# Relative attention: unshifted score rows are shifted from SBUF to SBUF, four partitions a transfer, instead of through a DRAM buffer

## The reference

```
AC = jnp.einsum('bhid,bhjd->bhij', q + u_bias[None, :, None, :], k)
BD = jnp.einsum('bhid,hjd->bhij', q + v_bias[None, :, None, :], rp)
BD = _rel_shift(BD)        # row i is moved left by an amount that depends on i
attn = jax.nn.softmax((AC + BD) * scale, axis=-1)
out = jnp.einsum('bhij,bhjd->bhid', attn, v)
```

## Time and profile before

| | |
|---|---|
| median of 3 runs | 2229.96 us (2224.44 to 2232.92) |
| profiled execution, its own time | 2224.83 us |
| its span | 2223.2 us |
| relative attention, first to last tile of DVE | 1202.6 to about 2079 us |
| one of its 32 steps | 27.4 us on average |

### The profile page before, as it was taken

The page is one execution under the profiler, slowest core; times in us unless marked ns, Lnnn a source line. Parts: engine busy times, 40 slices in busy tenths (PEclk is TensorE's granted clock), DMA queues, the critical chain, the costliest instruction groups (busy, mean ns, idle before and its releaser), DMA issues. The chain is left out here.

```text
span 2223.2 us, 56316 instructions
## 1 busy us (share of the span) xinstructions
PE 1591.8 (72%) x20267; PEld 1050.0 (47%) x20455; DVE 1321.3 (59%) x3147; ACT 1036.5 (47%) x1964; POOL 185.3 (8%) x281
## 2 busy tenths in 40 slices
PE   5433358788832999997624888787888787988547
PEld 2212136566621666664312555455555555656323
DVE  5764277566635666674321767576666665767546
ACT  4432226566620232321414767576666665766203
POOL 2322300000023000000210000000000000000013
PEclk8767669889965999998865989899998888989759
DMA  1114722222136212121789899999999999999441
GB/s 38 42 43 156 218 58 62 51 55 59 48 102 199 95 53 105 52 91 44 225 227 312 307 363 347 349 333 344 339 357 345 344 337 348 316 369 343 128 134 57
DMA packets 220937, 433.30 MB, mean 195 GB/s; under 512 B 54736, under 2 KB 116080, under 8 KB 211280
## 3 DMA queue, kind: packets, MB, share of 16 engines
q1 hardware_dynamic: 202928, 263.61, 39.4%
q10 hardware_dynamic: 12672, 152.05, 16.6%
q0 software_dynamic: 5088, 14.16, 2.1%
HBM read 225.93 MB, written 203.55 MB: 193 GB/s over the span
## 5 line engine op out<-in xcount | busy, mean ns | idle before, releaser
L2013 DVE CUSTOM_DVE_ANT_0 r_shifted<-r_ps_ac,r_shifted 128x512 f32<-128x512 f32 x512 | 352.1, 688 | 319.7 <-PE r_ps_ac L1890 157.5
L1979 ACT ACTIVATE r_probs<-r_ps_keys 128x512 f32<-128x512 f32 x512 | 309.6, 605 | 259.3 <-PE r_ps_keys L1897 225.8
L1897 PE MATMUL r_ps_keys<-r_ident,r_shifted 128*128 128x128 f32 x2048 | 334.0, 289 | 64.0 <-DMA r_v<-v 27.8
L1958 ACT ACTIVATE r_wide<-r_ps_wide 128x512 f32<-128x512 f32 (+1 forms) x576 | 329.7, 591 | 86.4 <-PE r_ps_wide L1881 85.0
L1897 PEld LDWEIGHTS r_ps_keys<-r_ident,r_shifted 128*128 128x128 f32 x2048 | 273.8, 149 | 54.2 <-issue 13.3
L1881 PE MATMUL r_ps_wide<-r_r,r_qv 48*32 48x64 bf16 (+12 forms) x6144 | 244.6, 259 | 65.7 <-issue 54.7
L2021 DVE TENSOR_SCALAR r_shifted<-r_shifted,r_mx 128x512 f32<-128x512 f32 x512 | 249.2, 487 | 18.3
L873 DVE TENSOR_REDUCE c_mx<-c_ps_rows 128x2 f32<-128x256 f32 (+3 forms) x256 | 197.7, 818 | 100.9 <-PE c_ps_rows L744 100.2
L846 ACT ACTIVATE c_probs<-c_ps_keys 128x512 f32<-128x512 f32 (+1 forms) x384 | 179.9, 530 | 140.6 <-PE c_ps_keys L744 137.2
L1881 PEld LDWEIGHTS r_ps_wide<-r_r,r_qv 48*32 48x32 bf16 x6144 | 105.9, 96 | 170.5 <-issue 168.7
L1357 ACT ACTIVATE e_silu<-e_ps_a 128x1024 f32<-128x1024 f32 x64 | 65.7, 1027 | 216.1 <-PE e_ps_a L1290 216.1
(11 more groups left out here) (197 smaller groups left out, 2084.5 us busy)
## 6 DMA issues: line engine op xcount, KB each, us to landing
skew<-r_wide ACTq DMA_DIRECT2D x64, 2224.0 KB, 12.1
r_shifted<-skew SPq DMA_DIRECT2D x64, 2048.0 KB, 18.3
e_weight_all<-weights SPq DMA_DIRECT2D x8, 2048.0 KB, 7.7
stack<-d_part SPq DMA_DIRECT2D x96, 128.0 KB, 2.6
stack<-b_part SPq DMA_DIRECT2D x48, 128.0 KB, 3.5
stack<-b_part POOLq DMA_DIRECT2D x48, 128.0 KB, 3.7
c_q<-stack SPq DMA_DIRECT2D x64, 96.0 KB, 2.2
c_k<-stack SPq DMA_DIRECT2D x64, 96.0 KB, 2.3
```

Source lines behind the costliest of these rows:

```text
L1897: last = pe.transpose(ps_keys[u % 2][:, j * P:(j + 1) * P], shifted[:, s, u, j * P:(j + 1) * P], ident[:, :])
L1958: act.activation(wide[:, s, c, lo:hi], ps_wide[bk % BANKS][:, 0:hi - lo], ACT.Copy).then_inc(wide_sb, 1)
L1979: act.activation(probs[:, h % 2, :, b * P:(b + 1) * P], ps_keys[u % 2][:, :].rearrange("p (j i) -> p j i", j=NT), ACT.Exp, scale=SCALE).th ...
L2013: dve.tensor_tensor_reduce(out=shifted[:, s, u, :], in0=ps_ac[u % 2][:, :], in1=shifted[:, s, u, :], scale=1.0, scalar=LOWEST, op0=ALU.add ...
```

## The change

The DRAM buffer goes. Each half of `wide` is copied by DMAs from SBUF to SBUF, straight into `shifted`. Rows at the same place i in the four strips (partitions i, i+32, i+64, i+96) need the same shift, so one transfer moves these four rows: 4 partitions x 8 tiles x 512 elements, 64 KB. A half takes 32 such transfers. SP's queue issues those of places 0, 16, 1, 17, ..., 7, 23, and GpSimd's queue those of places 8, 24, 9, 25, ..., 15, 31. GpSimd had no work in this phase before. Since the strips need no common pitch, their columns are no longer staggered, and `wide` has 4352 columns a half instead of 4448.

```
-CW = HT * W + P - Q
+    CW = HT * W
+    PLACES = [[i + o for i in range(Q // 4) for o in offsets] for offsets in ((0, 16), (8, 24))]
+    SKEW = 16 * Q // 2
+        tiles = wide[:, :, :, :].rearrange("p s c (v w) -> p s c v w", w=W)
...
+        def skew(eng, it, j, c, half, turned):
+
+            eng.wait_ge(wide_sb, 2 * NBK * (STEP * it + j) + NBK * (c + 1))
+            eng.sem_inc(skew_marks[half], 1)
+            if turned is not None:
+                eng.wait_ge(keys_ps, turned)
+                eng.sem_inc(skew_marks[half], 1)
+            for i in PLACES[half]:
+                at = Q - 1 - i
+                eng.dma_start(shifted[i::Q, j % 2, HT * c:HT * (c + 1), :], tiles[i::Q, j % 2, c, :, at:at + L])                    .then_inc(skewed[half][j % 2][c], 16)
+
+        def skew_step(eng, it, j, first, left, half):
+            n = STEP * it + j
+            if left >= 1:
+                skew(eng, *after(it, j, 1), 1, half, None if first else TG * n)
+            if left >= 2:
+                skew(eng, *after(it, j, 2), 0, half, TG * n + HT)
...
-            def fetch(it, j, c):
-
-                sp.wait_ge(sent[j % 2][c], 16 * uses(it, j))
-                src = skew_dram[j % 2][c]
-                sp.dma_start(shifted[:, j % 2, HT * c:HT * (c + 1), :],
-                             bass.AP(tensor=src.tensor, offset=src.offset + P - 1, ap=[[CW - 1, P], [W, HT], [1, L]]))\
-                    .then_inc(skewed[j % 2][c], 16)
...
-                if left >= 1:
-                    if not first:
-                        sp.wait_ge(keys_ps, TG * n)
-                    fetch(*after(it, j, 1), 1)
-                if left >= 2:
-                    sp.wait_ge(keys_ps, TG * n + HT)
-                    fetch(*after(it, j, 2), 0)
+                skew_step(sp, it, j, first, left, 0)
...
+        @block.gpsimd
+        def _(pool):
+            for c in range(2):
+                skew(pool, 0, 0, c, 1, None)
+            skew(pool, 0, 1, 0, 1, None)
+            steps(lambda it, j, first, left: skew_step(pool, it, j, first, left, 1), pool)
...
-                        start = W * v + P - Q - Q * a
+                        start = W * v
...
-            def send(n, s, c):
-                act.wait_ge(wide_sb, 2 * NBK * n + NBK * (c + 1))
-                dst = skew_dram[s][c]
-                act.dma_start(bass.AP(tensor=dst.tensor, offset=dst.offset, ap=[[CW, P], [1, CW]]),
-                              wide[:, s, c, :]).then_inc(sent[s][c], 16)
...
                         if bk == 0:
-                            act.wait_ge(sent[s][c], 16 * uses(it, j))
+                            for half in range(2):
+                                act.wait_ge(skewed[half][s][c], SKEW * uses(it, j))
...
                     if u % HT == 0:
-                        dve.wait_ge(skewed[s][u // HT], 16 * uses(it, j))
+                        for half in range(2):
+                            dve.wait_ge(skewed[half][s][u // HT], SKEW * uses(it, j))
```

More of the change, by code:

```diff
@@ L1704, in _, with phase_relative @@
             steps(step, dve)
-def phase_relative(nc, sems, qu_stacks, qv_stacks, k_stacks, v9_in, r_stack, ident_in, skew_dram, ctx_out):
+def phase_relative(nc, sems, qu_stacks, qv_stacks, k_stacks, v9_in, r_stack, ident_in, ctx_out):
     SCALE = DH ** -0.5
     BANK = 512
+    CW = HT * W
     NBK = -(-CW // BANK)
@@ L1754, in phase_relative @@
         wide_sb = sem("wide_sb")
-        sent = [[sem(f"sent{s}{c}") for c in range(2)] for s in range(2)]
-        skewed = [[sem(f"skewed{s}{c}") for c in range(2)] for s in range(2)]
+        skew_marks = [sem("skew_marks0"), sem("skew_marks1")]
+        skewed = [[[sem(f"skewed{half}{s}{c}") for c in range(2)] for s in range(2)] for half in range(2)]
         ac_ps = sem("ac_ps")
@@ L1781, in uses, with after @@
             return (STEP // 2) * it + j // 2 + 1
+        def after(it, j, by):
+            return it + (j + by) // STEP, (j + by) % STEP
+        def skew(eng, it, j, c, half, turned):
[13 more added lines that the diff above has]
+                skew(eng, *after(it, j, 2), 0, half, TG * n + HT)
         @block.sync
@@ L1795, in load_queries @@
                     .then_inc(qv_loaded[j % 2], 16)
-            def fetch(it, j, c):
-                sp.wait_ge(sent[j % 2][c], 16 * uses(it, j))
-                src = skew_dram[j % 2][c]
-                sp.dma_start(shifted[:, j % 2, HT * c:HT * (c + 1), :],
-                             bass.AP(tensor=src.tensor, offset=src.offset + P - 1, ap=[[CW - 1, P], [W, HT], [1, L]]))\
-                    .then_inc(skewed[j % 2][c], 16)
-            def after(it, j, by):
-                return it + (j + by) // STEP, (j + by) % STEP
             def step(it, j, first, left):
@@ L1841, in _ @@
             for c in range(2):
-                fetch(0, 0, c)
+                skew(sp, 0, 0, c, 0, None)
             sp.wait_ge(wide_ps, 2 * NBK)
             load_queries(0, 2)
-            fetch(0, 1, 0)
+            skew(sp, 0, 1, 0, 0, None)
             sp.wait_ge(wide_ps, 4 * NBK)
@@ L1853, in _ @@
                 for c in range(2):
-                    sp.wait_ge(sent[s][c], 16 * (NI // 2))
-                    sp.wait_ge(skewed[s][c], 16 * (NI // 2))
+                    for half in range(2):
+                        sp.wait_ge(skewed[half][s][c], SKEW * (NI // 2))
             sp.wait_ge(r_loaded, 32)
             sp.wait_ge(stored, 64 * (NI + 1))
+        @block.gpsimd
[4 more added lines that the diff above has]
+            steps(lambda it, j, first, left: skew_step(pool, it, j, first, left, 1), pool)
         @block.tensor
@@ L1988, in step @@
                             copy_wide(n + 2, s, c, HT)
-                            send(n + 2, s, c)
                     if u == 2 and not first:
@@ L1998, in _ @@
                         copy_wide(n, n, c, bk)
-                    send(n, n, c)
             steps(step, act)
@@ L2048, in program @@
     r_stack = dram("r_stack", (SK, H, 2 * L), BF16)
-    skew = [[dram(f"skew{s}_{c}", (P * CW,)) for c in range(2)] for s in range(2)]
     sems = Semaphores(nc)
@@ L2065, in program @@
     sems = Semaphores(nc, sems)
-    phase_relative(nc, sems, stacks[2], stacks[3], stacks[4], v9[1], r_stack, ident, skew, sums[1])
+    phase_relative(nc, sems, stacks[2], stacks[3], stacks[4], v9[1], r_stack, ident, sums[1])
     sems = Semaphores(nc, sems)
```

## The result

The changed kernel takes 2646.3 us (median of 4 runs, 2644.6 to 2652.6) against 2228.3 us before: 1.188 times, with a 95% interval of 1.183 to 1.193. The forecast was 2750 us, range 2260 to 3150. Slower was right, the size was 104 us too large. Full engines were rightly named, as the traces show, but they are not all that holds the kernel, and the prices of an issue and of GpSimd's traffic were wrong.

What follows compares the result with a forecast made beforehand. Transfers were taken to bound relative attention at 27.4 us a step. Four DMA engines with 701 KB at 16 GB/s give 43.8 us: 16.4 us more, x 32 = +525 on 2224.8, so 2750 us, range 2260 to 3150.

Steps and rivals of the forecast that it cites:

- What bounded the kernel before: Relative attention, 27.4 us a step, was held by its transfers (DMA engines 97% busy), mostly the detour through DRAM.
- What the change removes: 8.75 MB a step of DRAM write and read back, replaced by 4.19 MB; ACT's 21 us of issues worth nothing.
- No term: Stage's first tile: its new wait, 16 us for 1 MB through four engines, is about as long as write and fetch.
- Few DMA engines: A 4-partition transfer runs on 4 engines, the same four for all SP's transfers; each has 701 KB a step.
- Issuing: SP's 32 issues cost 9 to 13 us a step, GpSimd's 18.6 us, both inside the step.
- The rate: Each of the four engines moves 16 GB/s, hindered half of the time, so 701 KB take 43.8 us a step.
- rival 1: The four engines don't hinder each other: 29.2 us a step, +58 us, 2283 us; chance 0.17.
- the forecast's span: Steps between 29.2 us (engines unhindered) and 58.4 us (always hindering each other), given as 2286 to 3217 us.
- Sharing between partitions: Partitions 32 apart lie on one port; always in step, SP's half alone would take 38.5 us on two ports.
- 2: SP's transfers go round over all 16 engines; TensorE sets a 23.5 us step, -125 us, 2100 us; chance 0.17.
- 3: GpSimd's issues become the bound beside DVE's work; doubled to 1.16 us, 37.1 us a step, 2535 us; chance 0.07.
- The signs to look for: DMA share about a half, SP's landing times far beyond GpSimd's, DVE waiting for SP's half, step over 35 us.

Runs made afterwards that it cites:

- short transfers: Changed kernel with all 64 transfers a step issued, each moving 2 of its 8 tiles, 16 KB instead of 64 (scores wrong): 2101 us, 0.941 times.
- SP alone, 4 engines: Changed kernel without GpSimd's transfers, its places never shifted (scores wrong), SP's 32 transfers a step kept: 2323 us, 1.041 times.
- SP 8 places, GpSimd 24: Changed kernel with SP given 8 of the 32 places and GpSimd 24, right shifts: 2359 us, from one execution.
- GpSimd's transfers short: Changed kernel with GpSimd's 32 transfers a step cut to 2 of their 8 tiles, SP's whole (scores wrong): 2377 us, 1.069 times.
- another order of places: Changed kernel with SP's places ordered 0, 4, 16, 20, 1, ... and GpSimd's 8, 12, 24, 28, 9, ..., right shifts: 2479 us, 1.112 times.
- SP 12 places, GpSimd 20: Changed kernel with 12 places for SP, 20 for GpSimd, neighbouring transfers reaching other ports, right shifts: 2499 us, 1.120 times.
- partitions 4 apart: Changed kernel with SP's four partitions of a transfer 4 apart instead of 32, SP having places 0 to 15 (scores wrong): 2614 us, 1.172 times.
- SP's transfers on 16 engines: Changed kernel with each SP transfer reaching 16 partitions and 2 tiles instead of 4 and 8, still 64 KB (scores wrong): 2685 us, 1.204 times.
- the same, SP alone: SP's transfers of 16 partitions and 2 tiles, without any transfer of GpSimd (scores wrong): 2236 us, 1.006 times.

## Why the prediction was right, and where its reason failed

*What bounded the kernel before* stands: with few enough bytes (short transfers) the phase runs at 23.7 us a step instead of 27.4.

*What the change removes* stands: ACT did the same work in the same time, TensorE the same work in 1635 us instead of 1592, at a lower granted clock in this stage (0.76 instead of 0.89). The other phases hardly moved: the span grew by 421.8 us, of which 404.4 lie between DVE's first and last tile (1279.9 against 875.5) and 19.7 before the first, at 1222.3 instead of 1202.6 us, and behind them it is 2.3 shorter. Those 19.7 are a small miss: the forecast had "No term" there.

*Few DMA engines* stands as a count, exactly, and these engines are full. The Trainium skill's rule ("DMA: Bandwidth & Descriptors", Why a DMA increments its semaphore by 16 and not by 1) agrees with the four completions a transfer and with a share of 0.25 while more transfers wait; no run shows which four engines they are. What the four have to do in a step can be estimated from the packet records of 1400 to 2000 us: the durations of SP's 2048-byte packets over the engines that they run on, and those of all other packets of SP's and GpSimd's queues over 16, as if evenly spread.

| kernel | packet time of each of SP's engines, us a step | step, us |
|---|---|---|
| SP alone, 4 engines | 30 | 30.6 |
| SP 8 places, GpSimd 24 | 37 | 31.6 |
| GpSimd's transfers short | 33 | 32.2 |
| another order of places | 40 | 35.3 |
| SP 12 places, GpSimd 20 | 42 | 36.0 |
| partitions 4 apart | 46 | 39.1 |
| the changed kernel | 48 | 40.0 |
| SP's transfers on 16 engines | 26 | 41.0 |
| the same, SP alone | 11 | 27.9 |

In the first seven the packet time is about the step or over it (so packets must overlap in the records), as full engines would show, and with both queues' transfers whole a longer packet time goes with a longer step. It is no independent price, since the time of a packet of one size changes with the traffic beside it (GpSimd's 4 KB take 329 to 489 ns here). In the last two the engines are not full on average; the step is no shorter beside GpSimd's traffic, and 2.7 us shorter without it. So the forecast named a load that is there, but taking it away does not give a fast kernel; what then holds SP's queue stays open.

*Issuing* is a step that failed: "SP's 32 issues cost 0.28 us ... to 0.39 us: 9 to 13 us a step, inside the step". The rows that it rested on were other shapes. A 4 x 8 x 512 transfer takes 0.59 us from issue to issue, 18.9 us a step, and with the other issues SP's queue has 23.7 us of work of its own, as much as TensorE. Push-back comes on top of that at once; full engines and what hinders them have 16 us of the 40 us step to explain.

*The rate*: 16 GB/s for an engine was a guess for all traffic, and that 701 KB in 40.0 us are 17.5 GB/s is in part luck. Of the forecast's 43.8 us, SP's 524 KB were 32.8, and their packets took about 30; GpSimd's 131 KB were 8.2, and took about 14; loads and stores were 2.9, and took 3.6. The term that was mis-sized most is GpSimd's: 9.0 GB/s for a busy engine, near the lower bound of 8.9 from the earlier trace rows, where its half was given the same rate as SP's. In steps, the runs add up like this: 23.7 us for SP's queue with short transfers, + 6.9 for the length of SP's own transfers (SP alone, 30.6), + 9.4 for GpSimd's transfers beside them (40.0), of which 7.8 go with three quarters of their bytes; a better order of places gives back 4.7. How a full engine reaches back to the queue that issues is argued from these differences and from the DMA shares; the trace does not show it. A slip without weight: 29.2 us a step is 2283 us, as under rival 1, not the 2286 at the low end of the forecast's span.

*Sharing between partitions* matters where it was not looked for. Among SP's transfers it is worth 1.2 us a step as measured, with dearer issues against it; among GpSimd's, several of which are under way at once, busy engines run at 7.5 GB/s with nothing else beside them and at 11.2 in another order. That fits the Trainium skill's port map ("SBUF — State Buffer", Door 1: The DMA port swizzle): 32 apart is the same port, and places 8, 24, 9, 25 put four transfers on four ports, 8, 12, 24, 28 on eight. The runs show that the order matters; they don't show the ports.

*The rivals*: 1 (29.2 us a step) fell; near it is only the kernel with SP's half alone, 30.6. 2 fell: no spreading. 3 fell: GpSimd's issues stayed at 587 ns in the median and 852 at most beside DVE's work, and its queue stood idle 713 us. The signs to look for came true in part: the step over 35 us, POOL's issues near 0.6 us, a DMA share of 0.64 where a half was named. That DVE would wait for SP's half did not come true: the long wait is TensorE's, for loads behind SP's transfers. The forecast had that wait, with the reason that they are late only when the four engines are behind. The landing time of SP's transfers against GpSimd's could not be read; the profile gives none for these issues.

## What to carry to other kernels

Count a queue's own time like an engine's: issues of the very shape times their interval, plus all its other issues, and compare the sum with the step; a queue without a gap holds the step even when the mean DMA share is a third below full. Look at that share where one queue is alone: 0.25 of 16 engines can be four full ones. Look also at what else stands in the queue, here the next step's loads. Fewer bytes are no gain if they travel in transfers that reach few partitions: here a byte of GpSimd's cost twice the engine time of a 128-partition write. When small transfers can't be avoided, try other orders: places 8, 12, 24, 28 one after another instead of 8, 24, 9, 25 (and likewise on SP's queue) were worth 168 us here with no other change.

## What the runs showed of the hardware that was not expected

- The least cost of an issue on SP's queue depends on the pattern: 277 ns for 9 x 4 x 128 (SBUF to DRAM), 377 for 128 x 8 x 512 (DRAM to SBUF), 532 for 4 x 8 x 512 from SBUF to SBUF with partitions 32 apart (the same with 2 tiles instead of 8), 637 with partitions 4 apart.
- GpSimd's queue: 1024 transfers of 64 KB made 87008 - 5088 = 81920 packets, 80 each, most of them under 512 B, where SP's made 36 each. Its issues took 587 ns in the median in the changed kernel and never more than 852 ns, while SP's took up to 6.3 us.
- The push-back falls on whatever stands next in the queue, loads to 16 engines too: the loads of `k` took 1.4 us to issue in the median, 0.5 before the change:

```profile
L1811 SPq DMA_DIRECT2D r_k<-stack x32: 367/1382/3002, 1165.5 to 2472.1; - x32
```
